# Twelve fields of every quad get eight single-row fetches on ScalarE, and GpSimd gathers three tiles fewer

## The reference

```python
B, N_DENSE, N_FIELDS, VOCAB, EMBED_DIM, ATT_DIM = (2048, 13, 26, 12500, 32, 8)
emb = tables[field, sparse[:, field]]             # (B, 26, 32)
bi = emb[:, FIRST, :] * emb[:, SECOND, :]         # (B, 325, 32), all pairs of fields
a = relu(einsum('bpd,dh->bph', bi, att_w_w) + att_w_b)
scores = einsum('bph,ho->bpo', a, att_d_w) + att_d_b
att_weight = softmax(scores, axis=1)              # over the 325 pairs
att_out = sum(att_weight * bi, axis=1)
out = sigmoid(concat([att_out, dense]) @ fin_w + fin_b)
```

## Time and profile before

| | us |
|---|---|
| median of three runs | 463.36 |
| lowest, highest | 462.75, 465.7 |
| the profiled execution | 462.11 |
| its span, first to last instruction | 460.3 |
| mean granted TensorE clock | 0.961 of full speed |

### The profile page before, as it was taken

One profiled execution on the slowest core, in us unless ns is written; L12 is line 12 of the kernel. 1 busy time (PEld: TensorE's weight loads), 2 busy tenths in 40 slices (PEclk: granted clock), 3 DMA queues, 4 the chain that ended last, 5 costly groups with the idle time before them and its releaser, 6 DMA issues.

```text
span 460.3 us, 9277 instructions
## 1 busy us (share of the span) xinstructions
PE 393.7 (86%) x2508; PEld 225.5 (49%) x2508; DVE 394.7 (86%) x638; ACT 130.3 (28%) x305; POOL 332.4 (72%) x350
## 2 busy tenths in 40 slices
PE   0686969999999789699999859999999989869884
PEld 0575736553439566345427625554535957512122
DVE  4999898999988678899988669799988889786995
ACT  2303311232452111033263111124253211124353
POOL 5877777777777777777777777777777777777720
PEclk9979889999999899899999997999999999997999
DMA  8456422332223333222214242324121323222310
GB/s 285 105 152 117 73 14 26 18 25 15 14 14 27 26 16 24 14 26 16 16 15 25 15 25 14 27 16 25 15 15 15 15 14 16 13 15 13 17 7 1
DMA packets 16308, 15.44 MB, mean 34 GB/s; under 512 B 7952, under 2 KB 15360, under 8 KB 15872
## 3 DMA queue, kind: packets, MB, share of 16 engines
q0 software_dynamic: 11072, 5.69, 25.7%
q1 hardware_dynamic: 2800, 6.79, 4.1%
q10 hardware_dynamic: 2384, 2.37, 1.6%
HBM read 14.79 MB, written 0.02 MB: 32 GB/s over the span
## 4 chain that ended last, share of the span: by engine, by line
POOL 66%; issue 22%; PE 4%; DMA 4%; DVE 3%; ACT 1%; POOLq 0%; DVEq 0%; ACTq 0%
POOL emb L437 65%; DMA emb<-tables,rows 3%; PE first L488 2%; PE sums_f L498 1%; PE sums_s L512 1%; DVE ring L876 1%; DVE onehot L776 0%; DMA ids<-sparse 0%; PE back L536 0%; POOL emb_placed L426 0%; DVE emb_t L852 0%; ACT shared L624 0%; ACT shared L618 0%; POOLq L177 0%; DVE look_masked L861 0%
## 5 line engine op out<-in xcount | busy, mean ns | idle before, releaser
L437 POOL DMA_INDIRECT emb<-tables,rows x300 | 283.6, 945 | 91.5 <-issue 90.3
L876 DVE TENSOR_TENSOR ring<-emb_t,turned 128x512 f32<-128x512 f32 (+9 forms) x180 | 191.7, 1100 | 0.3
L471 PE MATMUL looked_own<-look_parts,onehot 128*128 128x448 f32 x546 | 124.3, 379 | 10.2 <-DVE look_masked L861 6.3
L471 PEld LDWEIGHTS looked_own<-look_parts,onehot 128*128 128x128 f32 x546 | 103.4, 194 | 35.5 <-issue 23.9
L488 PE MATMUL first<-ring,par 128*32 128x512 f32 (+1 forms) x672 | 89.7, 607 | 31.0 <-DVE ring L876 30.6
L605 ACT ACTIVATE hidden<-first,par 128x512 f32<-128x512 f32 (+1 forms) x84 | 56.5, 678 | 173.2 <-PE first L488 172.0
L498 PE MATMUL sums_f<-ring,par 128*32 128x512 f32 (+1 forms) x672 | 92.4, 601 | 0.0
L471 PE MATMUL back<-look_parts,onehot 128*128 128x448 f32 x350 | 81.2, 385 | 10.1 <-issue 5.4
L471 PEld LDWEIGHTS back<-look_parts,onehot 128*128 128x128 f32 x350 | 67.7, 198 | 27.7 <-issue 14.8
L852 DVE STREAM_TRANSPOSE emb_t<-emb 128x128 f32<-128x128 f32 x100 | 29.9, 302 | 40.1 <-DMA emb<-tables,rows 31.4
L776 DVE TENSOR_TENSOR onehot<-chunk_of,turned 128x896 fp32r<-128x896 f16 x60 | 63.1, 1051 | 0.1
(11 more groups left out here) (76 smaller groups left out, 129.6 us busy)
## 6 DMA issues: line engine op xcount, KB each, us to landing
emb_placed<-tables SPq DMA_DIRECT2D x768, 0.1 KB
emb<-tables,rows POOLq DMA_INDIRECT x300, 3.6
ring<-tables SPq DMA_DIRECT2D x2, 1568.0 KB, 7.7
shared<-tables SPq DMA_DIRECT2D x1, 1568.0 KB, 9.3
chunk_of<-chunk_numbers ACTq DMA_DIRECT2D x12, 128.0 KB, 3.4
ring<-tables SPq DMA_DIRECT2D x1, 896.0 KB, 6.7
emb<-tables,rows_first POOLq DMA_INDIRECT x44, 4.2
ring<-tables SPq DMA_DIRECT2D x1, 672.0 KB, 8.2
```

What stands on the lines that cost most here:

```text
L437: pool.indirect_dma_start(emb[:, f, g * D:(g + 1) * D], None, stacked, bass.IndirectOffsetOnAxis(ap=row, axis=0), element_offset=at,).then ...
L471: mm = nc.tensor.matmul(looked_rows[look_bank[tile]], onehot[:, tile % ONEHOTS, c, :], look_parts[:, n, c, k, :], start=c == 0 and k == 0, ...
L876: nc.vector.tensor_tensor(slot[:, at:at + n, :], emb_t[:, i:i + n, :], turned[f % 2][:, 0, :].unsqueeze(1).broadcast_to((P, n, P)), ALU.mu ...
```

## The change

Of field 24 the last three tiles of each quad are now placed ones (`PLACED` = 3), twelve in all. SyncE fetches the same six tiles. ScalarE fetches one tile for each of quads two, three and four (`TILES_ACT`), 384 rows. GpSimd gathers the other three (`BY_POOL` = 2, 0, 0, 1) at field 13 of the first quad, and one tile instead of two at field 24 of every quad: 343 gathers instead of 346.

ScalarE's rows are spread in bursts of eight (`ROWS_ACT`) over fields 9 to 20 of quad one and 1 to 12 of the others (`ROW_FIELDS`). In such a field, after copy f+1, it loads eight row numbers into registers and issues four rows; after the relus and bank copies of the field it issues the other four. The first 16 bursts are the tile of quad two, the next 16 that of quad three, the last 16 that of quad four.

```diff
-PLACED = 2
+TILES_ACT = (0, 1, 1, 1)
+ROWS_ACT = 8
+ROW_FIELDS = (range(9, 21), range(1, 13), range(1, 13), range(1, 13))
+PLACED = 3
...
+    BY_POOL = [PLACED - TILES_SP[q] - TILES_ACT[q] for q in range(QUADS)]
+    act_quads = [q for q in range(QUADS) if TILES_ACT[q]]
+    act_bursts = [(q, f) for q in range(QUADS) for f in ROW_FIELDS[q]]
...
-                            for i in range(PLACED - TILES_SP[n]):
+                            for i in range(BY_POOL[n]):
...
                 def place_rows():
-                    act.wait_ge(placed_gathered, (QUADS * PLACED - sum(TILES_SP)) * 16)
+                    act.wait_ge(placed_gathered, sum(BY_POOL) * 16)
+                    if TILES_ACT[q]:
+                        act.wait_ge(act_gathered[act_quads.index(q)], P * 16)
...
+                def load_row_numbers(f):
+
+                    if (q, f) not in act_bursts:
+                        return None
+                    row = act_bursts.index((q, f)) * ROWS_ACT
+                    if row == 0:
+                        act.wait_ge(sp_rows_ready, 1)
+                    to = act_quads[row // P]
+                    t = to * G + G - PLACED + BY_POOL[to]
+                    _, at = nc.values_load_multi_w_load_instructions(
+                        sp_rows[t:t + 1, row % P:row % P + ROWS_ACT], engines=(mybir.EngineType.Activation,), min_val=0,
+                        max_val=F * V - 1, skip_runtime_bounds_check_because="rows are clamped to their table")
+                    return row, at
+
+                def fetch_rows(burst, half):
+                    if burst is None:
+                        return
+                    row, at = burst
+                    to, i = act_quads[row // P], BY_POOL[act_quads[row // P]]
+                    for k in range(half * ROWS_ACT // 2, (half + 1) * ROWS_ACT // 2):
+                        p = row % P + k
+                        act.dma_start(emb_placed[p:p + 1, to, i * D:(i + 1) * D], stacked[bass.ds(at[k], 1), :]
+                                      ).then_inc(act_gathered[row // P], 16)
...
                     copy_turned(f + 1)
+                    burst = load_row_numbers(f)
+                    fetch_rows(burst, 0)
...
                             scores_home(FULL - 1)
+                    fetch_rows(burst, 1)
```

More of the change, by code:

```diff
@@ L120, in attention_fm @@
     PLACED_COLS = slice((G - PLACED) * D, G * D)
-    assert FIRST_FIELDS <= SP_FIRST < SP_PLACE < SP_FIELD and len(TILES_SP) == QUADS and max(TILES_SP) <= PLACED
+    assert FIRST_FIELDS <= SP_FIRST < SP_PLACE < SP_FIELD and len(TILES_SP) == QUADS
     assert SP_FIELD not in LOOK
+    BY_POOL = [PLACED - TILES_SP[q] - TILES_ACT[q] for q in range(QUADS)]
+    assert min(BY_POOL) >= 0 and max(TILES_ACT) == 1
+    act_quads = [q for q in range(QUADS) if TILES_ACT[q]]
+    act_bursts = [(q, f) for q in range(QUADS) for f in ROW_FIELDS[q]]
+    assert len(act_bursts) * ROWS_ACT == len(act_quads) * P and P % ROWS_ACT == 0
+    for k, q in enumerate(act_quads):
+        assert act_bursts[(k + 1) * P // ROWS_ACT - 1] < (q, SP_PLACE)
     assert G * D == P and B % (P * G) == 0 and RING < GROUPS and 1 < END_GROUPS
@@ L282, in attention_fm @@
         sp_gathered = [sem(f"sp_gathered{i}") for i in range(sum(TILES_SP))]
+        act_gathered = [sem(f"act_gathered{i}") for i in range(sum(TILES_ACT))]
         placed_gathered = sem("placed_gathered")
@@ L575, in _ @@
         def _(act):
+            stacked = tables.rearrange("f v d -> (f v) d")
             act.dma_start(par[:, cols["offset"]], params[:, cols["offset"]]).then_inc(offsets_in, 16)
```

## The result

The changed kernel takes 470.28 us (median of 4 runs, 468.87 to 470.95), the kernel before 463.11 (4 runs). The medians differ by 7.2 us, 1.5%; the ratio taken over all these runs is 1.0139, with a 95% interval of 1.0094 to 1.0183, so the kernel is slower, and by more than the noise. The profiled execution took 469.86, its span is 468.1. Forecast was 474, in a range of 460.5 to 499.

The account below looks back on a forecast made before the run. Gathers bound each quad's first half and VectorE its second; bursts make ScalarE's instruction stream the bound. 8.2 + 2.3 + 2.3 + 1.5 - 3.3 = +11.0 us on 462.11 gives 473.1, 474 in the median's terms; range 460.5 to 499.

Parts of the forecast that it names:

- The signs that the prediction named: VectorE's transpositions wait for copies instead of DMAs; gathers still start each 1.25 us and end at about 437.
- GpSimd gives 2.5 us, not 3.75: Three gathers fewer, 1.25 us each; only savings of quads two and three act: at most 2.5 us, 0.5%.
- the third saving: Quad four's saved gather, 1.25 us, lies behind its field 23, where nothing waits for gathers any more.
- The burst: ScalarE's load of eight registers, 0.69 us, and eight rows at 0.414: 4.0 us, ends 3.6 and 5.4.
- estimated 0.97, and 487 us: With the skill's 600 ns load floor, eight registers take 0.97 us, a burst 4.3, the kernel about 487.
- The stretches: ScalarE's stream outgrows the burst fields: quad one +8.2 us, quads two and three +2.3 each, quad four +1.5.
- the 1.3 at field 10: Quads two to four: the relu waits for TensorE's look-up with half a burst behind it, 1.3 us more.
- The end: Quad four's gather waits at fields 17, 18 and 23 vanish as VectorE comes late: 3.3 us given back.
- A: Bursts fit in ScalarE's waits, not slower: 461 us, or within 1% up to a burst of about 3.85; chance 0.35.
- My crossing point of 3.85 us: Up to a ScalarE burst of about this length, the time stays within 1%.
- B: ScalarE's register load is mostly fixed, 1.0 of 2.07 us: burst 4.6, kernel 503 us; chance 0.14.
- C: ScalarE and SyncE hinder each other at issuing: 0.06 us a row, 0.5 a burst, kernel 498 us; chance 0.07.

Follow-up runs that it names:

- run 3: Changed kernel with its 384 single-row DMAs at addresses fixed at the build, without register loads: 460.59 us, 0.9947 to the kernel before.
- run 5: Changed kernel with each burst's eight row numbers loaded as four and four, each load before its own rows: 497.28 us, 1.0714 to the kernel before.
- run 6: Changed kernel with each burst cut to its load of eight and one row by register, plus a plain DMA per tile: 460.95 us, 0.9946 to the kernel before.
- run 9: Changed kernel with each burst's halves in two successive fields, after copy f+1, over all fields 1 to 25 (quad four to 20): 460.76 us, 0.9945.
- run 2: Changed kernel without its 384 single-row DMAs, one plain DMA per tile instead; the build dropped the register loads too: 460.20 us, 0.9943 to the kernel before.
- run 7: Changed kernel without bursts in quad one and in quad four's fields 9 to 12, 32 bursts left, 344 gathers: 461.98 us, 0.9966 to the kernel before.
- run 8: Changed kernel with all eight rows of a burst at the field's end, behind relus and bank copies: 474.09 us, 1.0217 to the kernel before.
- run 10: As run 6, with a single-row DMA of fixed address between the load and the row by register: 459.94 us in one run.

## Why the prediction was right

**Direction and mechanism.** Slower by ScalarE's instruction stream: shown by runs 3, 5, 6 and 9, which change the stream's length or its place. The signs that the prediction named came: VectorE waits for copies, no longer for DMAs, and gathers go on every 1.25 us, the last one beginning at 436.95.

**GpSimd gives 2.5 us, not 3.75.** Ceiling kernels: 2.8, 2.4 and 2.1 us (runs 2, 3 and 6, each with an interval of some 0.9 to either side). It agrees. That the third saving is the hidden one was not tried by itself, but the traces fit: in these runs the last gather begins 3.1 to 3.8 us earlier than before (440.27 there), and the span ends only 1.9 to 2.5 earlier.

**The burst.** Forecast 0.69 + 8 x 0.414 = 4.0; measured 4.1. The load takes 0.744, a row 0.39 from start to start (235 ns, then 155 for register operation, move and gaps), and the first row's 0.234 was not foreseen. Rows that cost less than forecast made good what the load and the first row cost more, so that the burst came out right to 0.1 us is in part luck. Loads of 4, 8 and 32 take 0.509, 0.744 and 2.15: 0.058 us for a register and 0.28 fixed. By the floor that the Trainium skill gives for a load ("DMA: Bandwidth & Descriptors", "Latency and other measured facts") I had estimated 0.97, and 487 us; the load of four in run 5, at 0.509, is below that floor. The measurement decides.

**The stretches.** Quad one +8.2 forecast, +9.1 measured between the ends that I took, +8.6 from start to start (I read 113.86 as the start of field 22's block, and it is where VectorE began to wait). Quads two and three +2.3, measured +2.2 and +1.8; quad four +1.5, measured +0.9. The small terms of these sums, such as the 1.3 at field 10, were not measured one by one.

**The end: the mis-sized term.** I let the last stretch give back 3.3 us, the gather waits at fields 17, 18 and 23. It gave 5.6. Set side by side, most of the rest lies at one place, the transposition that waits for copy 20: 3.05 us before, 1.02 after.

```profile
423.69 0.31 DVE L852 STREAM_TRANSPOSE emb_t<-emb 128x128 f32<-128x128 f32 x1 [3.05 <-ACT turned L672]
```

```profile
431.94 0.31 DVE L895 STREAM_TRANSPOSE emb_t<-emb 128x128 f32<-128x128 f32 x1 [1.02 <-ACT turned L712]
```

Copy 20 stands behind the bank copies of fields 16 and 17 and so behind TensorE, and in the profiled execution of before TensorE was slow just there. Its timeline at field 17, and two stretches:

```profile
413.17 1.06 PE L488 MATMUL first<-ring,par 128*32 128x512 f32 x8 [2.58 <-DVE ring L876]
```

```profile
414.00:417.00 3.00, 2.10 (x16) 0.33 (x12) 2.01 (x4) 1.46 (x3) 2.36 (x3) 0.54 0.16 11
417.00:421.00 4.00, 4.00 (x20) 1.11 (x16) 3.63 (x4) 1.28 (x2) 3.09 (x4) 0.50 0.33 13
```

The granted clock (the third last number) is 0.54 and 0.50, the lower level, 1.2 GHz, after TensorE had waited 2.58 us for pairs; in the changed kernel the same work ran at 1.00, 2.4 GHz. Why the clock fell in the one and not in the other was not tried.

But the slow clock isn't what the end gave back. Run 6 shows the same end without it:

```profile
403.32:458.38 55.06, 37.49 (x318) 11.06 (x314) 43.52 (x74) 21.72 (x52) 26.43 (x28) 0.97 0.19 10
409.00:424.00 15.00, 10.63 (x88) 2.96 (x92) 12.10 (x14) 5.91 (x12) 11.35 (x13) 1.00 0.24 13
```

```profile
419.85 0.31 DVE L899 STREAM_TRANSPOSE emb_t<-emb 128x128 f32<-128x128 f32 x1 [1.04 <-ACT turned L716]
...
430.34 0.33 DVE L897 STREAM_TRANSPOSE turned<-emb 128x128 f32<-128x128 f32 x1 [1.22 <-DMA emb<-tables,rows]
...
435.06 0.33 DVE L897 STREAM_TRANSPOSE turned<-emb 128x128 f32<-128x128 f32 x1 [1.02 <-DMA emb<-tables,rows]
```

The clock is 1.00 at these fields and the wait for copy 20 is 1.04, and still the last stretch takes 55.06 us, against 55.16 before: VectorE waits for gathers at fields 22 and 23 instead, 1.22 and 1.02, beside 2.08 and 0.86 at 17 and 18. Runs 2 and 3 take 55.4 and 55.1. So up to field 23 the gathers set the pace of the end, and in the profiled execution of before the slow clock used up waits that VectorE would have had for them anyway. Where VectorE comes late, in the changed kernel and in runs 5, 7 and 8, the last stretch takes 49.5 us. The step that was mis-sized is the term -3.3: I added up the waits for gathers that the one trace shows. What a late VectorE gives back is the whole stretch as the gathers pace it, less VectorE's own 49.5, and that is 5.6. I read the page for waits and not the clock behind them, and so didn't see that one wait stood in for others.

**The rivals.** A: at the price of 2.2 us (run 3) or 1.4 (run 6) a burst does fit in the waits, as A has it; the real burst didn't. My crossing point of 3.85 us was not measured. But A's idea was good where I had not looked: with the same rows and loads in halves over all fields, only quad one's early fields lose, and the gather waits behind them take that up, as A has it (run 9). B: the load is 0.28 fixed, not 1.0. C: SyncE's rows kept their 225 ns median and 304 at most beside 384 rows of ScalarE, and ScalarE's 235; forecast by C was 0.06 us more for each row. The Trainium skill's lock on the descriptor generator ("Perfetto Trace Analysis", "DMA Instruction — HWDGE (DVE, Sync)") leaves at most a trace: of ScalarE's 48 first rows after a load five took 527 to 552 ns, and these five began 10 to 39 ns after a row of SyncE; none of the other 336 rows took over 256. SyncE's last row for quad three ended at 319.6, at 319.7 before.

## What to carry to other kernels

An engine that is busy 28% can be the bound: issuing DMAs and loading registers is not busy time, so add up its instruction stream by stretch, and compare it with the length of that stretch, not of the kernel. The price of small work put beside other work is a threshold: below it nothing, above it every tenth of a microsecond times the number of places, so halve the portion and use twice the places. A delay that arises early is paid only if the engines behind it have no waits left to make it good, so don't put the new work into just the stretches that hold these waits. A wait in one trace can stand in for another one, so size what a late engine gives back by the whole stretch, not by the waits that you see. And when a test is made by adding or dropping an instruction, count it in the trace first.

## What the runs showed of the hardware

- The first single-row DMA that ScalarE issues after a register load takes about 468 ns instead of 235 (48 of 48 in the changed kernel), also with a fixed address (462 ns, run 10), and also after 384 us, when SyncE has stopped issuing. A DMA of 128 rows in that place took 339 to 358 ns in run 10, 339 to 341 without loads in run 2. On SyncE the first row after a load of 32 registers takes 260 instead of 225 ns.
- A register load takes 0.28 us and 0.058 for each register (4 and 8 of them on ScalarE, 32 on SyncE; one line fits all three).
- A single-row DMA by register costs ScalarE 0.39 us of its stream; with an address fixed at the build, with nothing between, mostly 0.26 to 0.31.
- Two engines that issue 384 and 768 single-row DMAs side by side don't slow each other down beyond a few cases: the medians stay at 225 ns on SyncE and 235 on ScalarE, and five of ScalarE's rows took 527 to 552 where 468 was usual.
